# Attention on one core: the five mixing rounds of a set spread over its four steps, and a separate signal for finished denominators

## What is computed

```python
qk = jnp.einsum('bceqd,bcekd->bceqk', q, k) / math.sqrt(h)
a = jax.nn.softmax(qk, axis=-1)
o = jnp.einsum('bceqk,bcekd->bceqd', a, v)
...
return _conv(_mcl(o, Wo, bo), o_conv_w, o_conv_b, 0)
x = x + _L0_conv_ref(_gn(x), ...)
x = x + _L1_conv_ref(_gn(x), L1_conv_weight, L1_conv_bias)
```

## Time and profile before

| | us |
|---|---|
| median of three timed runs (1251.6 to 1258.3) | 1254.8 |
| profiled execution | 1258.8 |
| its span | 1256.9 |
| TensorE, GpSimd, VectorE, ScalarE busy | 1079.0, 871.2, 933.5, 663.2 |
| mean granted TensorE clock | 0.963 of full |

### The profile page before, as it was taken

How to read it: one execution, slowest core, us unless ns; L and a number is a source line. 1 busy time by engine, 2 the same in 40 slices (tenths; PEclk the granted TensorE clock), 3 DMA queues, 4 the chain that set the end, 5 groups by cost and what they waited for, 6 DMA issues and landing times. The chain is left out here.

```text
span 1256.9 us, 26231 instructions
## 1 busy us (share of the span) xinstructions
PE 1079.0 (86%) x10648; PEld 590.9 (47%) x10648; DVE 933.5 (74%) x1225; ACT 663.2 (53%) x1110; POOL 871.2 (69%) x812
## 2 busy tenths in 40 slices
PE   0299999999894699899998999999988589899998
PEld 0177777777673123333333333333333345355553
DVE  3789999999764798788888888888872584544344
ACT  1555555555442066666666666666666223346345
POOL 0467776777583489899998899988999007937900
PEclk9899999999998589999999999999999799899999
DMA  9725244332644555527171736254000599875661
GB/s 305 238 83 161 76 124 116 104 94 67 139 105 99 115 77 126 111 55 116 49 121 35 122 65 114 57 94 81 31 19 18 184 354 299 265 228 155 190 214 54
DMA packets 137759, 159.02 MB, mean 127 GB/s; under 512 B 17852, under 2 KB 85708, under 8 KB 137640
## 3 DMA queue, kind: packets, MB, share of 16 engines
q1 hardware_dynamic: 113448, 119.37, 39.6%
q10 hardware_dynamic: 15648, 28.81, 6.6%
q0 software_dynamic: 8544, 9.18, 2.8%
HBM read 106.48 MB, written 52.89 MB: 127 GB/s over the span
## 5 line engine op out<-in xcount | busy, mean ns | idle before, releaser
L1108 POOL TENSOR_TENSOR a_pl<-a_prob 128x512 bf16<-128x512 f32 x416 | 443.1, 1094 | 37.0 <-ACT a_prob L1059 36.4
L1012 DVE TENSOR_REDUCE a_negmax<-a_row 128x1 f32<-128x512 f32 x512 | 334.1, 706 | 60.4 <-PE a_row L939 59.2
L1059 ACT ACTIVATE a_prob<-a_col 128x512 f32<-128x512 f32 x512 | 292.1, 596 | 147.0 <-PE a_col L960 140.7
L710 POOL TENSOR_TENSOR f_yl<-f_y,f_yh 128x768 bf16<-128x768 f32 x80 | 132.8, 1679 | 95.8 <-ACT f_yh L657 95.8
L657 ACT ACTIVATE f_yh<-f_y 128x768 bf16<-128x768 f32 x80 | 67.4, 844 | 139.1 <-DVE f_y L548 121.2
L1023 DVE TENSOR_TENSOR a_pl<-a_prob 128x512 bf16<-128x512 f32 x96 | 123.3, 1285 | 19.2 <-ACT a_prob L1059 19.2
L450 PE MATMUL f_acc<-f_wh,f_xh 128*32 128x384 bf16 x1280 | 110.9, 335 | 29.8 <-DVE f_wl L538 26.5
L939 PE MATMUL a_row<-k,q 96*128 96x512 bf16 x256 | 106.6, 423 | 22.7 <-PEq L202 14.9
L960 PE MATMUL a_col<-a_q,a_k 98*128 98x512 bf16 x256 | 97.9, 388 | 23.2 <-ACT a_prob L1059 19.3
L960 PE MATMUL a_col<-q,k 98*128 98x512 bf16 x256 | 99.8, 390 | 16.1 <-ACT a_prob L1059 14.7
L714 POOL TENSOR_TENSOR f_straight<-f_straight,f_turned 128x832 f32<-128x832 f32 x40 | 107.0, 2675 | 9.4 <-DVE f_turned L565 9.4
(11 more groups left out here) (156 smaller groups left out, 2189.2 us busy)
## 6 DMA issues: line engine op xcount, KB each, us to landing
X<-b_x ACTq DMA_DIRECT2D x16, 526.0 KB, 8.3
q<-in_x SPq DMA_DIRECT2D x8, 1024.0 KB, 7.7
a_v<-V SPq DMA_DIRECT2D x16, 512.0 KB, 4.4
Z<-a_z ACTq DMA_DIRECT2D x32, 256.0 KB, 3.5
b_z<-Z SPq DMA_DIRECT2D x16, 512.0 KB, 11.0
b_x<-in_x SPq DMA_DIRECT2D x32, 256.0 KB, 10.1
b_res<-X SPq DMA_DIRECT2D x38, 208.0 KB
out<-b_y ACTq DMA_DIRECT2D x38, 208.0 KB
```

What stands on the lines that cost most here:

```text
L710: nc.gpsimd.tensor_tensor(yl[half][n % 2][:], y[half][:], yh[half][n % 2][:], ALU.subtract).then_inc(yl_done, 1)
L1012: nc.vector.reduce_max(negmax[n % PAIR][:, 0, t:t + 1], row[step % ROWS][:], AX.X, negate=True).then_inc(max_done, 1)
L1059: nc.scalar.activation(prob[sets_done % RING][:, t % QUAD, :], col[step % 2][:], ACT.Exp).then_inc(exp_done, 1)
L1108: nc.gpsimd.tensor_tensor(pl[p][:, r, :], prob[p][:, r, :], ph[p][:, r, :], ALU.subtract).then_inc(lo_pool, 1)
```

## The change

`mix_set` becomes `mix_round`: the five rounds j = 0 to 4 of a set (ones with `ph`, ones with `pl`, `vh` with `ph`, `vl` with `ph`, `vh` with `pl`) are given slots of their own by `ROUNDS`. Counted from the slot of the old burst, a set with kt = 0 has rounds 0 and 1 in slot 1, 2 in slot 2, 3 and 4 in slot 3; kt = 1 and 2 have 0, 1, 2 and then 3 and 4; kt = 3 has 0, 1 and 2 in slot 0, 3 and 4 in slot 1. The waits for low parts and logs stand before round 0, those for V and for the last division before round 2. A new semaphore `weighed` is signalled by the second round of a quad's last set, and the log waits for it and no longer for `mixed`. The division moves one slot later (KEEP + 1) and the output parts too (TAIL is one more).

```diff
-        TAIL = KEEP + QUAD * QT + 2
+        TAIL = KEEP + QUAD * QT + 3
+        ROUNDS = [((), (0, 1), (2,), (3, 4))] + [((0,), (1,), (2,), (3, 4))] * (QT - 2) + [((0, 1, 2), (3, 4), (), ())]
...
-        def sets(first, emit):
-            return [(STEPS * n + first + QUAD * g, lambda n=n, g=g: emit(n, g)) for n in range(UNITS) for g in range(SETS)]
+        def rounds(first, emit):
+            return [(STEPS * n + first + QUAD * g + t, lambda n=n, g=g, j=j: emit(n, g, j))
+                    for n in range(UNITS) for g in range(SETS) for t in range(QUAD) for j in ROUNDS[g % QT][t]]
...
-            def mix_set(n, g):
+            def mix_round(n, g, j):
                 kt, quad = g % QT, SETS // QT * n + g // QT
                 p = (SETS * n + g) % RING
-                pe.wait_ge(lo_pool, pool_lows(n, g))
-                pe.wait_ge(lo_dve, dve_lows(n, g))
-                if n == g == 0:
-                    pe.wait_ge(ones_set, 1)
-                if kt == 0 and quad:
-                    pe.wait_ge(logged, quad)
...
+                if j == 0:
+                    pe.wait_ge(lo_pool, pool_lows(n, g))
+                    pe.wait_ge(lo_dve, dve_lows(n, g))
+                    if n == g == 0:
+                        pe.wait_ge(ones_set, 1)
+                    if kt == 0 and quad:
+                        pe.wait_ge(logged, quad)
+                if j == 2:
+                    if g == 0:
+                        pe.wait_ge(v_lo, n + 1)
+                    if kt == 0 and quad:
+                        pe.wait_ge(divided, quad)
+                part = (ph, pl, ph, ph, pl)[j]
+                for r in range(QUAD):
+                    h = g // QT * QUAD + r
+                    to, weights = (weight, ones[:]) if j < 2 else (mix, (vl if j == 3 else vh)[n % 2][:, kt, h * DH:(h + 1) * DH])
+                    last = nc.tensor.matmul(to[r * DH:(r + 1) * DH, :], weights, part[p][:, r, :],
+                                            start=kt == 0 and j in (0, 2), stop=kt == QT - 1 and j in (1, 4))
+                if j == 1 and kt == QT - 1:
+                    last.then_inc(weighed, 1)
+                if j == 4:
+                    last.then_inc(mixed, 1)
...
-            pipeline(units(TURN, turn_max) + steps(EXP, col_scores) + steps(0, row_scores) + sets(MIX, mix_set) + tail_parts(TAIL, tail))
+            pipeline(units(TURN, turn_max) + steps(EXP, col_scores) + steps(0, row_scores) + rounds(MIX, mix_round) + tail_parts(TAIL, tail))
...
-            pipeline(steps(0, row_max) + units(SPLIT, split_max) + lows(EXP + 1, low_part, False) + quads(KEEP, divide))
+            pipeline(steps(0, row_max) + units(SPLIT, split_max) + lows(EXP + 1, low_part, False) + quads(KEEP + 1, divide))
...
-                act.wait_ge(mixed, QT * (quad + 1))
+                act.wait_ge(weighed, quad + 1)
```

More of the change, by code:

```diff
@@ L798, in attend @@
         mixed = sem("a_mixed")
+        weighed = sem("a_weighed")
         logged = sem("a_logged")
```

## The result

The changed kernel takes 1296.5 us (median; 1293.0 to 1298.1), against 1253.5 us for the kernel before, measured beside it: ratio 1.033, 95% interval 1.030 to 1.037. The forecast was 1291.5 us, slower. The profiled execution took 1296.8 us, its span 1294.8 us, 37.9 us above the span before.

The account below looks back on a forecast made before the run. VectorE bounds the start; in the middle no engine is full, and TensorE's unit is 28.8 us of work plus 4.4 of stalls. +2.6 us in each of 14 units, +36.7 us, gives median 1291.5 us, range 1264 to 1305.

Parts of the forecast that it names:

- The switch: On TensorE, each of 18 further groups of rounds between full-width scores pays 0.19 us: +3.4 us a unit.
- rival B: On TensorE, only entering a group behind a wait costs; 16 of 26 groups enter free: 1271 us, chance 0.12.
- Output parts behind a round: On TensorE, 7 of a unit's eight output parts stand behind a round, before 2: 5 x 0.11 = +0.55 us.
- What leaves: TensorE's waits for exponentials (1.1 us a unit) and its wait behind the copy of V (1.07 us) go.
- small waits: TensorE's column scores waiting for exponentials after a burst, about 0.2 us in each of five sets: 1.1 us a unit, to go.
- First quad's end: TensorE still waits for ScalarE's log and what follows: 0.57 us in slot 6, 0.38 in slot 7, stall 0.95 us.
- Second quad's end: Output parts wait for the division, now behind VectorE's low part in slot 20: stall 2.1 us, before 0.38 + 0.86.
- Sum: Per unit of the middle: +3.4 + 0.55 - 4.4 + (0.95 + 2.1) = +2.6 us; 14 units, +36.7 us.
- Rival A: On TensorE, weight loads of isolated rounds hide under the scores: 31.9 us a unit, 1237 us, not slower; chance 0.10.
- Rival C: VectorE falls behind by a further low part (1.4 us) where low part and division meet: 1311 us, chance 0.10.
- Rival D: Over the whole kernel, gains and switches cancel: 1249 to 1261 us, chance 0.06.

Follow-up runs that it names:

- split burst: The kernel before with only the first two rounds of each burst put ahead of the same slot's row scores, 16 groups a unit instead of 8: 1275.1 us.

## Why the prediction was right

By its own steps, for one quiet unit:

- **The switch.** Forecast 18 x 0.19 = 3.4 us. In the middle of after, entries at full clock are 0.30 to 0.32, in groups with and without a wait, which also settles rival B, and exits 0.31 to 0.35. The split burst shows 0.21 a group, so 3.8 us. TensorE's own work is 36.1 - 3.1 (stalls, below) = 33.0 us, against 28.8 + 3.4 + 0.55 = 32.8. Two rules stood against each other. These traces go with the Trainium skill's TensorEngine Tiling (section Tiling Modes), that a changed mode drains TensorE: they show a price of 0.2 us in and out of each group. The pull-ahead of weight loads, from the Trainium skill's TensorE: Matmul & The Clock Gate (section Step-by-step: what each phase is for), was seen only between matmuls of one width.
- **Output parts behind a round.** 0.55 us, as forecast.
- **What leaves.** The wait behind the copy of V is gone, as forecast, and so are the small waits but one of 0.20 us. New and not forecast: row scores wait once for VectorE, 0.47 us (the profile gives 0.30 of it as idle, at 620.38). VectorE is late there because its low part from 617.69 on takes 2.04 us.
- **First quad's end.** Forecast 0.57 and 0.38, measured 0.56 and 0.41.
- **Second quad's end.** The order on VectorE and the wait were right, the size was not: 2.1 us forecast, 1.46 measured. Of the difference, 0.44 us is the low part, 1.43 us by the earlier trace rows, 0.99 us here; the other 0.2 us is the small wait named above, which falls just ahead and makes TensorE arrive later. GpSimd is busy all through that low part, so the prediction's two lengths, 0.60 beside an idle GpSimd and 1.43 beside a busy one, are not the only ones.
- **Sum.** Stalls 0.97 + 0.20 + 0.47 + 1.46 = 3.1 us, forecast 3.05; a quiet unit 36.13 us, forecast 35.8. That the misses of the last three points nearly cancel is luck.
- **Not in the sum.** Five units lose 1.56 us each at the 1.2 GHz level behind the wait for the division, 7.8 us together. Against that, one unit before took 36.1 us instead of 33.2, with 2.5 us of waiting for the DMA of the maxima in it, and that wait is gone; and two units after are 0.6 us shorter than quiet ones. So 44 us in the middle where 37 were forecast. Of these, 6 us did not reach the span, since the end of the attention and the last stage, both put at nothing, were shorter; by medians the kernel lost 43.

Rival A would have needed a group below 0.04 us; it costs 0.2. Rival C didn't come: the one new wait for VectorE is a third of it. Rival D didn't either: the kernel is 3.3% slower. Where the prediction was thin is the attribution. I put +2.1 us of stall against 1.24 before, and so made the switches almost the whole loss; the experiments give the later division and output parts as much of it as the spread. The sum was right since the spread's gains were counted in it.

## What to carry to other kernels

Matmuls on a quarter of the array's columns between full-width ones cost 0.2 us a group here, whatever the waits; before a burst is spread to feed a waiting engine, count the groups and what waiting is left to remove: the first eight further groups paid here, the next ten did not. An instruction moved by one slot lands among others of its engine: look at which of them comes first in the list, because half of this loss came from a division behind a low part that nobody was waiting for yet. And a signal's worth is that of what is queued behind its waiter: under 1% in one order, about 2% in another.

## What the runs showed that was not expected

Nearly the same stall of TensorE, 1.27 to 1.30 us of idle time before the first output part (1.08 in the first unit), was in nine units followed by matmuls every 0.22 us and in five by matmuls every 0.43 us (mean granted clock 0.55 in 631.2 to 635.0 us), at a price of 1.56 us. With the division first (0.3 us of idle time there) none of the units showed it. But that wait is not needed for it. With the old signal, output parts don't wait for the division, and one of the 14 units still took 39.1 us instead of 37.4: behind idle times of 0.65 and 0.84 us at the first quad's end (801.1 and 802.5 us) the clock was granted at 0.50 until about 809 us. What decides it, these runs don't tell.
